# Packing four 64-row products two by two, adding the bias on ScalarE and giving the second layer a third bank, in a graph network layer on one core

## What is computed

```python
h   = maximum(layernorm(x), 0)                        # x: 50000 x 256
agg = segment_sum(edge_attr, dst) / maximum(counts,1) # 25000 edges of 64 features
hid = relu(concat([agg, h]) @ W1 + b1)                # W1: 320 x 512
x   = x + hid @ W2 + b2                               # W2: 512 x 256
```

## Time and profile before

| | before |
|---|---|
| median of 3 runs | 1377.42 us (1375.92 to 1379.47) |
| the profiled execution: time | 1376.72 us |
| the profiled execution: span, first to last instruction | 1375.1 us |
| mean granted clock of PE | 0.990 |
| busy: PE, DVE, ACT, POOL | 1335.7, 1195.0, 695.8, 537.3 us |

### The profile page before, as it was taken

One profiled execution on the slowest core, in us unless ns is written; L12 is line 12 of the kernel. 1 busy time (PEld: TensorE's weight loads), 2 busy tenths in 40 slices (PEclk: granted clock), 3 DMA queues, 4 the chain that ended last, 5 costly groups with the idle time before them and its releaser, 6 DMA issues.

```text
span 1375.1 us, 29825 instructions
## 1 busy us (share of the span) xinstructions
PE 1335.7 (97%) x7076; PEld 1121.4 (82%) x7076; DVE 1195.0 (87%) x2965; ACT 695.8 (51%) x1281; POOL 537.3 (39%) x710
## 2 busy tenths in 40 slices
PE   2699999999999999999999999999999999999998
PEld 1588888888888888888888888888888888888887
DVE  6598989898898989898988989898989888898986
ACT  2354545555454545455555545454555555454543
POOL 4334343443434343434334343434343343434341
PEclk7999999999999999999999999999999999999999
DMA  3345455554545454545555454545455554545452
GB/s 91 97 114 143 111 138 117 133 126 123 131 118 138 110 146 110 140 115 134 122 128 131 119 134 115 145 107 143 113 136 119 131 129 120 131 118 141 110 127 57
DMA packets 422789, 168.78 MB, mean 123 GB/s; under 512 B 321076, under 2 KB 422390, under 8 KB 422776
## 3 DMA queue, kind: packets, MB, share of 16 engines
q1 hardware_dynamic: 421076, 166.67, 50.1%
q10 hardware_dynamic: 1700, 1.97, 0.6%
HBM read 66.30 MB, written 51.40 MB: 86 GB/s over the span
## 4 chain that ended last, share of the span: by engine, by line
PE 96%; DVE 1%; DMA 1%; SPq 1%; issue 0%; ACT 0%; POOL 0%; DVEq 0%; POOLq 0%
PE P L836 27%; PE P L816 14%; PE P L838 14%; PE P L818 13%; PE P L817 13%; PE P L825 6%; PE P L826 6%; PE PA L805 2%; PE PA L806 2%; DMA dst_w<-in_dst_dram 1%; DVE wb_lo L725 0%; SPq L263 0%; DVE wb_lo L724 0%; ACT HN L533 0%; SPq L286 0%
## 5 line engine op out<-in xcount | busy, mean ns | idle before, releaser
L836 PE MATMUL P<-w_both,H_hi 128*128 128x512 f32 x1568 | 560.0, 398 | 9.7 <-DVE H_lo L673 9.7
L559 ACT ACTIVATE H_hi<-P 128x512 fp32r<-128x512 f32 x392 | 233.7, 597 | 512.2 <-PE P L826 512.2
L838 PE MATMUL P<-w_both,H_lo 128*128 128x256 f32 x1568 | 441.4, 281 | 0.0
L673 DVE SCALAR_TENSOR_TENSOR H_lo<-P,H_hi 128x512 fp32r<-128x512 f32 x392 | 269.2, 687 | 115.5 <-ACT H_hi L559 105.7
L836 PEld LDWEIGHTS P<-w_both,H_hi 128*128 128x128 f32 x1568 | 295.4, 188 | 83.0 <-DVE H_lo L673 11.0
L816 PE MATMUL P<-HT_hi,w_hi 128*128 128x512 f32 x784 | 314.3, 401 | 4.2 <-DVE HT_lo L665 4.2
L818 PE MATMUL P<-HT_hi,w_lo 128*128 128x512 f32 x784 | 308.9, 394 | 0.0
L817 PE MATMUL P<-HT_lo,w_hi 128*128 128x512 f32 x784 | 306.1, 390 | 0.0
L838 PEld LDWEIGHTS P<-w_both,H_lo 128*128 128x128 f32 x1568 | 295.0, 188 | 3.8
L433 POOL TENSOR_TENSOR XB<-X,b_row 128x1024 f32<-128x1024 f32 x98 | 236.6, 2415 | 136.1 <-DVE O L684 136.1
L427 POOL TENSOR_TENSOR E_lo<-ES,E_hi 128x256 fp32r<-128x256 f32 x98 | 73.2, 746 | 410.7 <-ACT E_hi L539 410.7
(11 more groups left out here) (76 smaller groups left out, 1136.4 us busy)
## 6 DMA issues: line engine op xcount, KB each, us to landing
X<-in_x_dram SPq DMA_DIRECT2D x97, 512.0 KB, 3.6
HQ<-HN SPq DMA_DIRECT2D x388, 128.0 KB, 3.1
out_dram<-O SPq DMA_DIRECT2D x97, 512.0 KB, 3.3
ER<-in_edge_attr_dram SPq DMA_DIRECT2D x392, 32.0 KB, 1.8
DT<-table_dram SPq DMA_DIRECT2D x392, 1.0 KB, 1.7
X<-in_x_dram ACTq DMA_DIRECT2D x1, 512.0 KB, 6.3
w_raw<-in_L_gnn_W_dram ACTq DMA_DIRECT2D x4, 128.0 KB, 5.9
w_raw<-in_L_gnn_W_dram ACTq DMA_DIRECT2D x2, 256.0 KB, 7.9
```

Of the source, the lines that this page charges most:

```text
L559: act.activation(H1_hi[:, m, :], bank(m)[:], ACT.Relu).then_inc(s_1hi, 1)
L673: dve.scalar_tensor_tensor(out=H1_lo[:, m, :], in0=bank(m)[:], scalar=0.0, in1=H1_hi[:, m, :], op0=ALU.max, op1=ALU.subtract).then_inc(s_1 ...
L836: pe.matmul(out_bank(j)[:], H1_hi[:, m, rows], w2_both[:, m, :, :].rearrange("p a d -> p (a d)"), start=(m == 0), stop=False)
L838: last = pe.matmul(out_bank(j)[:, 0:D], H1_lo[:, m, rows], w2_both[:, m, 0, :], start=False, stop=(m == CH - 1))
```

## The change

- The product of the means' high part and the low weight, which had 128 rows with the bias in half of them, now has 64 rows. For blocks m = 0 and 2 it uses array rows 0 to 63 (`QA`), for m = 1 and 3 array rows 64 to 127 (a copy of the high means, `QC`). `layer1_halves`, called after m = 1, issues m = 0 and 1 as one pair and then m = 2 and 3 as another. The second pair opens banks 2 and 3, whose node products come behind it; the first pair closes banks 0 and 1.
- The wait for the residual of tile t-1 (`s_fin`, for all four row groups) stands once, ahead of the four products.
- ACT adds the bias: each Relu gets `bias=b1_col[:, m:m+1]`, and a second Relu with the same bias writes the result back to the bank (`s_1`). `hidden_low` waits for both and is a plain subtraction.
- Layer 2's third row group goes to the bank `PS`, the fourth to `bank(3)`; the order is j0, j1, j2 with m 0 to 2, then m 3 of the three, then j3.
- At the start the rows of the bias and their splits go; the bias is loaded as a column for each block.

```diff
-            return (P2 + P1)[j]
+            return (P2[0][:], P2[1][:], PS[:].rearrange("p a b -> p (a b)"), bank(CH - 1)[:])[j]
...
-            act.wait_ge(s_const, 8)
-            for p in (64, 96):
-                act.dma_start(b1_raw[p:p + 1, :], b1.rearrange("(o h) -> o h", o=1)).then_inc(s_w[2], 16)
+            act.dma_start(b1_col[:], b1.rearrange("(m p) -> p m", p=P),
+                          allow_slow_non_contiguous=True).then_inc(s_w[2], 16)
...
-                act.activation(QB[0:DE, :], PA[0:DE, :], ACT.Copy).then_inc(s_qhi, 1)
+                act.activation(QA[0:DE, :], PA[0:DE, :], ACT.Copy).then_inc(s_qhi, 1)
                 act.wait_ge(s_qhi, 2 * t + 1)
-                act.activation(QA[0:DE, :], QB[0:DE, :], ACT.Copy).then_inc(s_qhi, 1)
+                act.activation(QC[DE:P, :], QA[0:DE, :], ACT.Copy).then_inc(s_qhi, 1)
...
-                    act.activation(H1_hi[:, m, :], bank(m)[:], ACT.Relu).then_inc(s_1hi, 1)
+                    act.activation(H1_hi[:, m, :], bank(m)[:], ACT.Relu, bias=b1_col[:, m:m + 1]).then_inc(s_1hi, 1)
+                    act.activation(bank(m)[:], bank(m)[:], ACT.Relu, bias=b1_col[:, m:m + 1]).then_inc(s_1, 1)
...
                 dve.wait_ge(s_1hi, CH * t + m + 1)
-                dve.scalar_tensor_tensor(out=H1_lo[:, m, :], in0=bank(m)[:], scalar=0.0, in1=H1_hi[:, m, :],
-                                         op0=ALU.max, op1=ALU.subtract).then_inc(s_1lo, 1)
+                dve.wait_ge(s_1, CH * t + m + 1)
+                dve.tensor_tensor(H1_lo[:, m, :], bank(m)[:], H1_hi[:, m, :], ALU.subtract).then_inc(s_1lo, 1)
...
-            dve.wait_ge(s_whi, 3)
-            dve.tensor_tensor(wb_lo[0:DE, :], wa_raw[0:DE, :], wa_hi[0:DE, :], ALU.subtract).then_inc(s_wblo, 1)
-            dve.tensor_tensor(wb_lo[96:P, :], b1_raw[96:P, :], b1_hi[96:P, :], ALU.subtract).then_inc(s_wblo, 1)
+            dve.wait_ge(s_whi, 2)
+            dve.tensor_tensor(wb_lo[:], wa_raw[:], wa_hi[:], ALU.subtract).then_inc(s_wblo, 1)
...
-                if m >= 2:
-                    past(pe, s_fin, SUB * (t - 1) + m + 1)
                 cols = slice(m * P, (m + 1) * P)
+                first = m < 2 or (isinstance(t, int) and t == 0)
...
-                pe.matmul(bank(m)[:], wa_hi[:, cols], QA[:], start=False, stop=False)
-                pe.matmul(bank(m)[:], wb_lo[:, cols], QB[:], start=False, stop=True).then_inc(s_l1, 1)
+                last = pe.matmul(bank(m)[:], wa_hi[:, m * P:(m + 1) * P], QA[:], start=False, stop=(m >= 2))
+                if m >= 2:
+                    last.then_inc(s_l1, 1)
+
+            def layer1_halves(t):
+
+                past(pe, s_fin, SUB * t)
+                for m in range(0, CH, 2):
+                    first = m == 2 and not (isinstance(t, int) and t == 0)
+                    one = pe.matmul(bank(m)[:], wb_lo[0:DE, m * P:(m + 1) * P], QA[0:DE, :], start=first, stop=(m == 0))
+                    two = pe.matmul(bank(m + 1)[:], wb_lo[DE:P, (m + 1) * P:(m + 2) * P], QC[DE:P, :],
+                                    start=first, stop=(m == 0))
+                    if m == 0:
+                        one.then_inc(s_l1, 1)
+                        two.then_inc(s_l1, 1)
...
-                for j, ms in ((0, (0, 1, 2)), (1, (0, 1, 2)), (0, (3,)), (1, (3,)), (2, (0, 1, 2, 3)), (3, (0, 1, 2, 3))):
+                for j, ms in ((0, (0, 1, 2)), (1, (0, 1, 2)), (2, (0, 1, 2)), (0, (3,)), (1, (3,)), (2, (3,)),
+                              (3, (0, 1, 2, 3))):
...
-                    if m == 1 and later and not (isinstance(t, int) and t == 0):
-                        edge_means(t + 1, 1 - b)
+                    if m == 1:
+                        layer1_halves(t)
+                        if later and not (isinstance(t, int) and t == 0):
+                            edge_means(t + 1, 1 - b)
```

More of the change, by code:

```diff
@@ L88, in build @@
         wa_raw = sb("wa_raw", [P, H])
-        b1_raw = sb("b1_raw", [P, H])
+        b1_col = sb("b1_col", [P, CH])
         w2_raw = sb("w2_raw", [P, CH, D])
@@ L94, in build @@
         wb_lo = sb("wb_lo", [P, H], F32R)
-        b1_hi = sb("b1_hi", [P, H], F32R)
         w2_both = sb("w2_both", [P, CH, 2, D], F32R)
@@ L142, in build @@
         QA = sb("QA", [P, TILE], F32R)
-        QB = sb("QB", [P, TILE], F32R)
+        QC = sb("QC", [P, TILE], F32R)
         H1_hi = sb("H1_hi", [P, CH, TILE], F32R)
@@ L194, in build @@
         s_rise = sem("s_rise")
-        s_ones = sem("s_ones")
+        s_1 = sem("s_1")
         s_target = sem("s_target")
@@ L381, in _ @@
             pool.memset(alike[:, 0:1], 0.0).then_inc(s_const, 1)
-            pool.memset(b1_raw[:], 0.0).then_inc(s_const, 1)
             pool.memset(ident[:], 0.0).then_inc(s_const, 1)
-            pool.wait_ge(s_const, 9)
+            pool.wait_ge(s_const, 8)
             pool.affine_select(out=ident[:], in_=ident[:], compare_op=ALU.not_equal, fill=1.0, base=0,
@@ L402, in _ @@
                       allow_small_or_imprecise_dtypes=True).then_inc(s_const, 1)
-            pool.wait_ge(s_const, 13)
+            pool.wait_ge(s_const, 12)
             pool.iota(base[:, TILES - 1, :], pattern=[[P, SUB]], base=LAST, channel_multiplier=0,
@@ L439, in _ @@
             pool.tensor_tensor(w1_lo[:], w1_raw[:], w1_hi[:], ALU.subtract).then_inc(s_wlo, 1)
-            pool.wait_ge(s_whi, 5)
+            pool.wait_ge(s_whi, 3)
             pool.tensor_tensor(w2_both[:, :, 1, :], w2_raw[:], w2_both[:, :, 0, :], ALU.subtract).then_inc(s_wlo, 1)
@@ L566, in _ @@
             act.activation(wa_hi[:], wa_raw[:], ACT.Copy).then_inc(s_whi, 1)
-            act.wait_ge(s_w[2], 32)
-            act.activation(b1_hi[DE:P, :], b1_raw[DE:P, :], ACT.Copy).then_inc(s_whi, 1)
-            act.activation(wb_lo[64:96, :], b1_raw[64:96, :], ACT.Copy).then_inc(s_whi, 1)
+            act.wait_ge(s_w[2], 16)
             act.wait_ge(s_w[3], 32)
@@ L622, in _ @@
             dve.memset(dst_w[96:EP, HALO + ER_:WIDE], 1 << 20).then_inc(s_wide, 1)
-            dve.memset(QB[DE:P, :].bitcast(F32), 1.0).then_inc(s_ones, 1)
             dve.wait_ge(s_dst, 16)
@@ L668, in means_low @@
                 dve.wait_ge(s_qhi, 2 * t + 1)
-                dve.tensor_tensor(QA[DE:P, :], PA[0:DE, :], QB[0:DE, :], ALU.subtract).then_inc(s_qlo, 1)
+                dve.tensor_tensor(QA[DE:P, :], PA[0:DE, :], QA[0:DE, :], ALU.subtract).then_inc(s_qlo, 1)
             def hidden_low(t, m):
                 dve.wait_ge(s_1hi, CH * t + m + 1)
-                dve.scalar_tensor_tensor(out=H1_lo[:, m, :], in0=bank(m)[:], scalar=0.0, in1=H1_hi[:, m, :],
-                                         op0=ALU.max, op1=ALU.subtract).then_inc(s_1lo, 1)
+                dve.wait_ge(s_1, CH * t + m + 1)
+                dve.tensor_tensor(H1_lo[:, m, :], bank(m)[:], H1_hi[:, m, :], ALU.subtract).then_inc(s_1lo, 1)
             def residual(t, b, j):
@@ L731, in _ @@
             with dve.If(flag != 0):
-                dve.wait_ge(s_const, 14)
+                dve.wait_ge(s_const, 13)
                 dve.wait_ge(s_starti, 1)
@@ L811, in layer1_nodes @@
                     pe.wait_ge(s_hlo, 2 * t + 2)
-                if m >= 2:
-                    past(pe, s_fin, SUB * (t - 1) + m + 1)
                 cols = slice(m * P, (m + 1) * P)
+                first = m < 2 or (isinstance(t, int) and t == 0)
                 for c in range(CD):
-                    pe.matmul(bank(m)[:], w1_hi[:, c, cols], HT_hi[:, c, :], start=(c == 0), stop=False)
+                    pe.matmul(bank(m)[:], w1_hi[:, c, cols], HT_hi[:, c, :], start=(c == 0 and first), stop=False)
                     pe.matmul(bank(m)[:], w1_hi[:, c, cols], HT_lo[:, c, :], start=False, stop=False)
@@ L834, in layer2 @@
                             pe.wait_ge(s_1lo, CH * t + m + 1)
-                        pe.matmul(out_bank(j)[:], H1_hi[:, m, rows], w2_both[:, m, :, :].rearrange("p a d -> p (a d)"),
+                        pe.matmul(out_bank(j), H1_hi[:, m, rows], w2_both[:, m, :, :].rearrange("p a d -> p (a d)"),
                                   start=(m == 0), stop=False)
@@ L841, in layer2 @@
                         last.then_inc(s_l2, 1)
-                    if j == 2 and isinstance(t, int) and t == 0:
+                    if j == 2 and m == CH - 1 and isinstance(t, int) and t == 0:
                         edge_means(1, 1)
@@ L855, in _ @@
             flag = pe.value_load(flag_i[0:1, 0:1], min_val=0, max_val=1 << 20)
-            pe.wait_ge(s_const, 10)
+            pe.wait_ge(s_const, 9)
             for j in range(SUB):
@@ L877, in _ @@
             pe.wait_ge(s_wlo, 2)
-            pe.wait_ge(s_ones, 1)
-            pe.wait_ge(s_wblo, 2)
-            pe.wait_ge(s_whi, 5)
+            pe.wait_ge(s_wblo, 1)
+            pe.wait_ge(s_whi, 3)
             step(0, 0)
```

1 line of the change is left out of this document (removed).

## The result

The changed kernel takes 1439.22 us (1438.69 to 1439.69, 4 runs), the kernel before 1377.11 us beside it: a ratio of 1.045, with an interval of 1.0437 to 1.0464. It is 62 us slower; 1452 was forecast, in a range of 1428 to 1485. The profiled execution's span is 1438.1 us, 63.0 more than before, or 0.65 us for each of 97 tiles.

What follows compares the result with a forecast made beforehand. A loop through DVE was taken as the bound: 12.42 + 1.89 = 14.31 us a tile. Start 63.3, 95 tiles 1359.5, tile 96 13.1 and end 13.9 sum to 1449.8, forecast as 1452 us; range 1428 to 1485.

Steps and rivals of the forecast that it cites:

- The loop: DVE's last residual, PE's first half product, ACT's two Relus, DVE's next tile: 14.1 to 14.4 us a tile; chance 0.68.
- the hand-over: From DVE's last residual over PE's product and ACT's two Relus to DVE's first `H1_lo`: 1.89 us, DVE idle.
- DVE's stretch: DVE's fixed order from the first `H1_lo` to the last residual of a tile: 12.42 us, one wait taken off.
- the start: Before tile 1: fewer subtractions and Relus, but a table's DMA is waited for; taken as 0, tile 1's half products at 63.30.
- The packed products: Half products of a pair run together on PE; rival that they don't, or shape changes drain: 1460 to 1478 us, chance 0.13.
- the two changes of shape: PE entering and leaving the 64-row array shape at the half products: 0.05 us for both together.
- the offset: Delay between the starts of the two half products of a pair on PE: taken as 0.05 us.
- The row from the edge means: First PE product behind the edge means reaches its successor after 0.28 us instead of 0.23: 0.05 for a shape change.
- PE's tile: PE's work in a tile: 13.52 - 0.92 + 0.56 = 13.16 us, inside the loop with 1.15 us to spare.
- PE as the bound at 1341 us: Rival: PE still sets the time and the saved products show, needing a loop of at most 13.16 us; chance 0.05.
- A dear write-back: Rival: ACT's write to PSUM costs up to 1.05 us a tile more, 1478 to 1550 us; chance 0.08.
- The clock: Rival: PE's clock falls in the new waits, three a tile; far above 1480 us, chance 0.03.

Runs made afterwards that it cites:

- the serial run: Changed kernel with all four half products in array rows 0 to 63, so that no two can stand together: 1481.72 us, ratio 1.0757.
- the split run: Changed kernel with the second pair and its wait behind the edge means, and the means' low part first in DVE's order: 1406.79 us, ratio 1.0213.

## Why the prediction was right

**The loop** was the cause, in the place where the prediction put it. The wait, the hand-over and DVE's idle time are in every tile of the trace, and the runs leave no other cause: taking the wait from the first pair gives back 22 us, taking the write-back out of the hand-over 61, filling the hand-over with other work 61, and the write-back without the wait costs nothing in the new order of layer 2.

**The hand-over** was put at 1.89 us and measured 1.94: PE 0.06 and 0.50 as said, the step between the two Relus 0.58 for 0.57, the write-back 0.65 for 0.69, and then 0.11 to DVE's start where 0.03 was taken.

**DVE's stretch** was put at 12.42 us and is 12.26. This term was mis-sized, and most of the difference in time comes from here: 0.16 us less, with 0.05 more for the hand-over, make 14.31 - 14.20 = 0.11 us a tile; in 95 tiles that is 10 of the 13 us between 1452 and 1439. Two more came at the start, which the prediction had put at nothing, between a gain of 2.7 and none: tile 1 reached its half products at 61.32 and not at 63.30.

```profile
61.32 0.50 PE L826 MATMUL P<-QA,wb_lo 64*128 64x512 f32 x1
```

The stretch had been read from the kernel before with one wait taken off. It held 0.15 us more of waiting, because a low part's row begins 0.08 us before that of the statistics ahead of it ends, and a wait shorter than that is shown nowhere. The run without write-back shows the 0.66 us step; it isn't the plain subtraction that is faster.

**The packed products**: they run together, so that rival is out, and the price of that rival, 14.4 to 14.6 us a tile, was measured by the serial run at 14.64. But the two changes of shape, put at 0.05 together, and 0.05 for the offset, cost 0.35 in one visit. The row from the edge means, from which both 0.05 were taken, was a poor neighbour. The drain that the Trainium skill (TensorEngine Tiling (Array Packing), Key Properties) states fits the trace: the 0.16 us for each change that the prediction had worked out and set aside, 0.32 together, are within 0.03 of it, though the rows divide it otherwise (0.10 into the pair, 0.20 from the pair to the edge products, 0.05 behind the first of these). It did not change the time, since PE had the slack; it does change what there was to win: PE's tile is 13.41 us and not 13.16, 11 us of 1377 in all.

**The rivals of the other sign**: PE as the bound at 1341 us needed a hand-over of 0.74 us and a tile of 13.16, and neither holds. A dear write-back is out: 657 ns. The clock stayed at its upper level, 0.989 granted in the mean against 0.990 before.

**Small steps that were off**: counted from start to start, beyond the 0.23 us of a product, PE loses 0.55 us at the half products (699.58 to 700.36; 0.10 of it is the change of shape), as forecast, 0.24 at the means (711.71 to 712.41) and not 0.3, and 0.10 in layer 2 (705.52 to 705.85) and not 0.2; with its work of 13.41 us this makes the 14.20. PE's share of the span is 95%, not 92, since the rows of matmuls ahead of a wait run into it.

**What stays open**: whether an order of DVE exists in which neither POOL's addition nor the third low part costs PE anything, so that the 11 us show.

## What to carry to other kernels

When a wait is moved ahead on one engine, look for the first instruction of the other engine that now depends on it: if it stands right behind the one that is waited for, in a fixed order, two engines that overlapped take turns, and the hand-over between them is paid in every round. Price the visit to another shape of the array before packing small products: here it took 0.35 of the 0.46 us that the two pairs save. Look also at what an instruction that is moved will stand beside: four columns on DVE took 2.37 us beside POOL. And when a stretch of an engine's work is read from a trace, subtract waits from start to start, since rows overlap and hide the short ones.

## What was not expected of the hardware

- **DVE beside POOL.** With POOL's addition of 128x1024 running (2.4 us), a DVE subtraction of 128x4 with both inputs in SBUF took 1.03 and 2.37 us instead of 0.15 in the tiles shown, and one-hot blocks 1.93 instead of 0.85 us for four; both went on only when POOL had ended, while statistics (0.74 for two) and products' low parts read from PSUM went on beside it undisturbed. The Trainium skill (SBUF — State Buffer, Who interferes with whom) says that a DVE instruction with two SBUF inputs contends with a GpSimd instruction that reads SBUF, and that `tensor_scalar` can; the runs agree.
- **Writing PSUM from ACT.** The write-back's row is 657 ns against 689 for the same Relu to SBUF, but DVE starts 0.11 us after its end and not 0.03. From start to the reader's start that is 0.76 us against 0.72: the chain is no shorter for the PSUM write, where the prediction had held some hundredths possible.
- **The array's shape.** 0.35 us for one visit to the 64-row shape and back, and 0.36 for the second visit of the split run, against 0.05 for the step from 128x64 back to 128x128.
